# Local attention layers: turned probabilities through a DRAM scratch, four wide reads in place of twelve SBUF copies, and new orders on all engines

## What is computed

```python
def attn_layer(x, Wqkv, qs, ksc, Wo):
    q, k, v = jnp.split(x @ Wqkv, 3, -1)          # 16 heads of 64
    q, k = l2norm(q) * qs, l2norm(k) * ksc
    q = q * cos * scale + rotate_half(q) * sin * scale
    k = k * cos * inv + rotate_half(k) * sin * inv
    out = local_attention(q, k, v)                # window of 64: softmax over this and the last window
    return out @ Wo
def ffn_layer(x, g, bln, W1, b1, W2, b2):
    a, gate = jnp.split((layernorm(x) * g + bln) @ W1 + b1, 2, -1)
    return a * jax.nn.gelu(gate, approximate=False) @ W2 + b2
for i in range(DEPTH):
    x = attn_layer(shift_tokens(x), Wqkv[i], q_scale[i], k_scale[i], Wo[i]) + x
    x = ffn_layer(shift_tokens(x), ln_g[i], ln_b[i], W1[i], b1[i], W2[i], b2[i]) + x
```

## Time and profile before

| | |
|---|---|
| median of 3 runs | 3710.45 us (3704.81 to 3710.89) |
| the profiled execution: time | 3711.28 us |
| the profiled execution: span | 3709.7 us |
| PE busy | 3492.5 us, 94% of the span |
| DVE busy | 2934.3 us, 79% |
| ACT busy | 2244.5 us, 61% |
| POOL busy | 2379.7 us, 64% |
| share of the chain that ended last | PE 62%, DVE 8%, SP's queue 2%, DMA 1% |

### The profile page before, as it was taken

How to read it: one execution, slowest core, us unless ns; L and a number is a source line. 1 busy time by engine, 2 the same in 40 slices (tenths; PEclk the granted TensorE clock), 3 DMA queues, 4 the chain that set the end, 5 groups by cost and what they waited for, 6 DMA issues and landing times.

```text
span 3709.7 us, 78239 instructions
## 1 busy us (share of the span) xinstructions
PE 3492.5 (94%) x25818; PEld 2453.3 (66%) x25818; DVE 2934.3 (79%) x9244; ACT 2244.5 (61%) x6802; POOL 2379.7 (64%) x2088
## 2 busy tenths in 40 slices
...
DMA packets 223105, 277.92 MB, mean 75 GB/s; under 512 B 60624, under 2 KB 184048, under 8 KB 221168
## 3 DMA queue, kind: packets, MB, share of 16 engines
...
q1 hardware_dynamic: 181600, 138.54, 13.1%
...
## 4 chain that ended last, share of the span: by engine, by line
PE 62%; DVE 8%; SPq 2%; issue 1%; POOL 1%; DMA 1%; ACT 0%; DVEq 0%; POOLq 0%; ACTq 0%
PE pj L1857 26%; PE y_ps L1912 9%; PE pj L1929 8%; PE y_ps L1938 7%; PE sc L1885 5%; PE o_ps L1902 4%; PE tp L1865 3%; DVE l_probs L2150 3%; SPq L1701 2%; DVE l_qk_cos L2112 2%; PE tp L1835 1%; DVE l_qT L2046 1%; DVE l_ss L2105 1%; DVE l_hT L2187 0%; DVE l_qk_sin L2114 0%
## 5 line engine op out<-in xcount | busy, mean ns | idle before, releaser
L1857 PE MATMUL pj<-w_qkv,l_xT 128*128 128x512 f32 x2304 | 1082.5, 603 | 48.3 <-DVE l_hT L2187 36.5
L1798 POOL TENSOR_TENSOR l_qk_rot<-l_qk_cos,l_qk_sin 128x512 f32<-128x512 f32 x376 | 580.1, 1543 | 688.3 <-DVE l_qk_sin L2115 565.9
L1857 PEld LDWEIGHTS pj<-w_qkv,l_xT 128*128 128x128 f32 x2304 | 408.5, 191 | 435.7 <-issue 376.6
L511 POOL DMA_INDIRECT f_rows<-in_emb,f_expert x512 | 505.4, 987 | 226.4 <-issue 144.9
L2001 ACT ACTIVATE l_probs<-l_probs,l_low 128x128 f32<-128x128 f32 x1536 | 595.0, 397 | 3.5 <-DVE l_low L2150 2.9
L1929 PE MATMUL pj<-l_xnT,l_w 128*128 128x256 f32 x2112 | 481.9, 380 | 1.2 <-issue 1.2
L1966 ACT ACTIVATE l_qk_raw<-pj 128x512 f32<-128x512 f32 x384 | 228.6, 595 | 398.6 <-DVE l_qk_sin L2115 276.1
L2150 DVE CUSTOM_DVE_ANT_0 l_probs<-sc,l_shut,l_r_q 128x128 f32<-128x128 f32 x1536 | 434.9, 339 | 29.7 <-PE sc L1885 29.0
L1929 PEld LDWEIGHTS pj<-l_xnT,l_w 128*128 128x128 f32 x2112 | 391.6, 191 | 50.6 <-issue 1.8
L1803 POOL TENSOR_TENSOR l_r_q<-l_ssm,l_minus_half 128x8 f32<-128x8 f32 x188 | 370.7, 1972 | 15.7
L2112 DVE TENSOR_TENSOR l_qk_cos<-l_qk_raw,l_rope 128x512 f32<-128x512 f32 x384 | 345.8, 900 | 0.0
...
## 6 DMA issues: line engine op xcount, KB each, us to landing
l_pT<-l_p_turned SPq DMA_DIRECT2D x1728, 32.0 KB, 1.8
w_qkv<-in_L_ffn_Wqkv SPq DMA_DIRECT2D x12, 1024.0 KB, 7.5
...
f_rows<-in_emb,f_expert POOLq DMA_INDIRECT x512
w_o<-in_L_ffn_Wo SPq DMA_DIRECT2D x6, 1024.0 KB, 5.5
w_qkv<-in_L_ffn_Wqkv SPq DMA_DIRECT2D x12, 512.0 KB, 4.9
l_xf<-l_stream SPq DMA_DIRECT2D x48, 128.0 KB, 2.3
```

Source lines behind the costliest of these rows:

```text
L511: pool.indirect_dma_start(rows[:, j % RH, k, :], None, dram["emb"], bass.IndirectOffsetOnAxis(ap=expert[:, n % 2, at:at + 1], axis=0)).the ...
L1798: pool.tensor_tensor(qk_rot[:, i % ROTS, :], qk_cos[:, b, :], qk_sin[:, b, :], ALU.add).then_inc(rotated if s == 0 else pool_front, 1)
L1857: last = pe.matmul(pj[b][:, :], xT[:, k, t * P:(t + 1) * P], w_qkv[:, k, s * INNER + c * 512:s * INNER + (c + 1) * 512], start=(k == 0), s ...
```

## The change

Three things change, all in `local_layers`.

1. The exchange. A new piece `park` writes a whole unit of `p_turned` (all 16 blocks, 512 KB, 4 KB from each of 128 partitions) into a DRAM scratch `parked`, by one DMA. `move` then waits for that DMA (`p_parked`) and reads the blocks back by four DMAs of 128 KB, each into 32 partitions. The zeroing of `pT` and the semaphore `cleared` are gone; masked blocks come as zeros out of the probabilities.
2. What waits for it. `turn` of unit u needs its slot of `p_turned` free: now as soon as the park of unit u - 2 has landed, before when its 12 moves had. `values` waits for 4 DMAs.
3. New lists for all five engines (and a new first pass for DVE). No piece is added or removed but the parks; pieces stand elsewhere.

```diff
-    MOVES = [(a, b, 0) for a, b in ((1, 0), (2, 0), (2, 1), (3, 1), (3, 2), (0, 0), (1, 1), (2, 2), (3, 3))]
-    MOVES += [(a, b, 1) for a, b in ((0, 2), (0, 3), (1, 3))]
-    MOVED = 16 * len(MOVES)
+    MOVED = 16 * 4
...
     ORDER["sync"] = [
-        ("move", 0, -1), ("load_qk", 0, 0), ("stage", 0, -2), ("move", 1, -1), ("load_2", 0, -1), ("load_o", 0, 0), ("load_v", 0, 0),
-        ("load_1", 0, 0), ("move", 2, -1), ("load_cols", 0, 0), ("move", 3, -1),
+        ("move", 0, -1), ("stage", 0, -2), ("park", 1, -1), ("move", 1, -1), ("load_qk", 0, 0), ("load_v", 0, 0), ("park", 2, -1), ("load_1", 0, 0),
+        ("load_2", 0, -1), ("move", 2, -1), ("park", 3, -1), ("load_o", 0, 0), ("move", 3, -1), ("load_cols", 0, 0), ("park", 0, 0),
     ]
...
+        parked = nc.dram_tensor("parked", (2, 4, BLOCK, 4, TILES * UH * BLOCK), F32, kind="Internal").ap()
...
-            def move(n, par, u):
+            def park(n, par, u):
                 sp.wait_ge(turned_32, UNITS * n + u + 1)
                 apart(sp, passed)
-                if n == 0 and u < 2:
-                    sp.wait_ge(cleared, 1)
+                wait(sp, moved[u % 2], MOVED * (2 * n + u // 2))
+                sp.dma_start(parked[u % 2].rearrange("a j b x -> (a j) (b x)"),
+                             p_turned[:, u % 2, :, :, :, :].rearrange("p b t h q -> p (b t h q)")).then_inc(p_parked[u % 2], 16)
+
+            def move(n, par, u):
+                sp.wait_ge(p_parked[u % 2], 16 * (2 * n + u // 2 + 1))
+                apart(sp, passed)
                 wait(sp, o_full, UNITS * n + u - 1)
-                for a, b, t in MOVES:
-                    sp.dma_start(pT[b * BLOCK:(b + 1) * BLOCK, u % 2, a, t:TILES, :, :],
-                                 p_turned[a * BLOCK:(a + 1) * BLOCK, u % 2, b, t:TILES, :, :]).then_inc(moved[u], 16)
+                for b in range(4):
+                    sp.dma_start(pT[b * BLOCK:(b + 1) * BLOCK, u % 2, :, :, :, :].rearrange("p a t h q -> p a (t h q)"),
+                                 parked[u % 2, :, :, b, :].rearrange("a j x -> j a x")).then_inc(moved[u % 2], 16)
...
-                    pool.memset(pT[:, :, :, :, :, :], 0.0).then_inc(cleared, 1)
...
-                pe.wait_ge(moved[u], MOVED * (n + 1))
+                pe.wait_ge(moved[u % 2], MOVED * (2 * n + u // 2 + 1))
...
-                before, unit = (n, u - 2) if u >= 2 else (n - 1, u + 2)
-                wait(dve, moved[unit], MOVED * (before + 1))
+                wait(dve, p_parked[u % 2], 16 * (2 * n + u // 2))
```

More of the change, by code:

```diff
@@ L1415, in local_layers @@
     ORDER["tensor"] = [
-        ("scores", 2, -1), ("project", 5, 0), ("project", 6, 0), ("qk_turn", 1, 0), ("project", 8, 0), ("wo", 0, -2), ("qk_turn", 3, 0),
-        ("project", 7, 0), ("project", 9, 0), ("scores", 3, -1), ("values", 0, -1), ("qk_turn", 2, 0), ("w1", 1, -3), ("w1", 2, -3),
-        ("qk_turn", 5, 0), ("project", 10, 0), ("qk_turn", 4, 0), ("project", 11, 0), ("xs", 0, 1), ("w1", 3, -3), ("w1", 4, -3), ("w1", 5, -3),
-        ("values", 1, -1), ("scores", 0, 0), ("project", 0, 1), ("project", 1, 1), ("qk_turn", 7, 0), ("project", 2, 1), ("xn", 0, -2),
@@ L1420, in local_layers @@
-        ("values", 2, -1), ("scores", 1, 0), ("qk_turn", 6, 0), ("project", 3, 1), ("w2", 0, -3), ("w2", 1, -3), ("qk_turn", 0, 1), ("w1", 0, -2),
-        ("project", 4, 1), ("values", 3, -1),
+        ("scores", 2, -1), ("project", 5, 0), ("project", 6, 0), ("qk_turn", 0, 0), ("qk_turn", 1, 0), ("wo", 0, -2), ("project", 8, 0),
+        ("project", 7, 0), ("qk_turn", 3, 0), ("project", 9, 0), ("qk_turn", 2, 0), ("w1", 1, -3), ("scores", 3, -1), ("values", 0, -1),
+        ("w1", 2, -3), ("project", 10, 0), ("qk_turn", 5, 0), ("project", 11, 0), ("qk_turn", 4, 0), ("xs", 0, 1), ("w1", 3, -3), ("w1", 4, -3),
```

43 lines of the change are left out of this document (23 added, 20 removed).

## The result

| | median | runs | profiled execution | its span |
|---|---|---|---|---|
| before | 3710.03 us | 3704.81 to 3710.89 | 3711.28 us | 3709.7 us |
| after | 3645.64 us | 3643.55 to 3649.63 | 3649.63 us | 3648.1 us |

The ratio is 0.9831, with an interval of 0.9814 to 0.9848: faster by 64 us. Forecast were 3658 us and a range of 3632 to 3700.

What follows compares the result with a forecast made beforehand. PE's own work was taken as the bound (busy 1291.4 of 1316 us), so only its losses between instructions could be won: 3711.3 - 13.5 - 35.1 - 0 - 4 = 3658.7, forecast 3658 us, range 3632 to 3700.

Steps and rivals of the forecast that it cites:

- Steps of 55.9 us: Local layers, `wo` to `wo`: each step falls from 57.0 to 55.9 us, 1.08 us won.
- `w1 1` ahead of `scores 3`, 35.1 us: Ahead of `project 10`: PE's wait for DVE's read-out mostly goes, 0.78 us a step, 35.1 us in 45 steps.
- the 0.29 that was left: Ahead of `project 10`: loss expected to remain each step, 0.19 us of wait plus 0.10 of slow restart.
- `project 8` behind `wo`, 13.5 us: `project 5`'s bank gets all of `wo` more for read-out, so 0.30 us a step goes, 13.5 us in 45 steps.
- The exchange hidden, 0 in the steps: From `turn 2` to `values 2`: 8.2 us of DRAM round trip fits into 11.9 us, 3.7 us of cover, no cost.
- the estimate of 3.2 us from its formula: The park's landing by the skill's formula: 2.0 us plus the bytes at 436 GB/s; the working took 3.7 us.
- the first rival: At `values 2`, every step: DRAM round trip late, slower kernel; 3897 us with landings like a 1024 KB load; chance 0.11.
- Layer ends net 0: Steps at layer ends: 5 us lost to late loads against 5 us of `pT` waits won, net 0.
- The 5 us allowed for a late `load_qk`: `project 0` of a new layer: weights late behind SP's wait for the park, 1 us in each of 5 steps.
- all 7.0 us for `pT`: Full steps' waits for `pT` where a load stands ahead of a `move`: 5 of the 7 us expected to go.
- First and last steps, 4 us: First and last steps: SP spends less time a unit, winning 1 us at the start and 3 at the end.

Runs made afterwards that it cites:

- lists_only: The kernel before with the five new lists, parks struck out, exchange still 12 SBUF copies a unit: 3668.48 us, ratio 0.9891.
- lists_with_old_sp: The kernel before with new lists on PE, DVE, ACT and POOL; SBUF copies and SP's list as before: 3764.95 us against 3805.37, ratio 0.9896.
- exchange_only: The kernel before with the DRAM exchange, old lists on all engines, each park right ahead of its move: 3733.57 us, ratio 1.0062.
- exchange_and_sp_list: The kernel before with the DRAM exchange and SP's new list, the other engines' lists old: 3801.58 us against 3805.37, ratio 0.9989.
- rotate7_between: The changed kernel with `rotate 7` between the two halves of `top 3` on DVE: 3843.92 us against 3805.37 for the kernel before, ratio 1.0096.
- turn5_first: The changed kernel with `qk_turn 5` ahead of `project 10` on PE: 3633.72 us, ratio 0.9795 to the kernel before.
- p8_before_wo: The changed kernel with `project 8` put back ahead of `wo` on PE: 3648.51 us, ratio 0.9835 to the kernel before.
- park_two: The changed kernel with one further 512 KB write to spare DRAM ahead of each park: 3672.64 us, ratio 0.9897 to the kernel before.
- park_five: The changed kernel with four further 512 KB writes to spare DRAM ahead of each park: 4042.68 us against 3805.37 for the kernel before, ratio 1.0613.
- lists_only_again: A repeat, in the third batch, of the kernel before with the new lists and no DRAM exchange: 3668.15 us, ratio 0.9891.
- lists_loads_up: New lists without the DRAM exchange, `load_qk` moved ahead of `move 1`, `load_cols` ahead of `load_o` and `move 3` on SP: 3655.56 us, ratio 0.9857.

## Why the prediction was right, and where it wasn't

- **Steps of 55.9 us.** Right, 55.93. All of it is the lists' (lists_only, lists_with_old_sp: 55.93 without the DRAM exchange; exchange_only, exchange_and_sp_list: 56.99 with it).
- **`w1 1` ahead of `scores 3`, 35.1 us.** Right in mechanism and size. 4.09 us from `scores 3` to `project 10` for 4.05; rotate7_between shows that DVE's order there is what PE waits for, and with turn5_first the step falls by 0.28 of the 0.29 that was left.
- **`project 8` behind `wo`, 13.5 us.** The size was right, the reason not the one that was needed. p8_before_wo takes the place away and loses nothing. The step of the working is "the bank of `project 5` has the whole of `wo` more to be read out in". That is true, but two things that the working left out are each enough without it: the bank is free 0.63 us earlier, since ACT's releaser on DVE is done sooner, and a second turn stands between. The working read PE's list for this place and not what ACT waits for. The three were not tried one by one, so which of them is needed stays open.
- **The exchange hidden, 0 in the steps.** Right: 8.0 us of round trip for 8.2, 4.3 us of cover for 3.7, and park_two's plain steps unchanged with another 512 KB in the way. Inside the round trip two misses cancel: from park to first read 3.6 us pass for 3.7, but from first read to last 1.3 for 2.1, and the last lands 3.0 us later for 2.3. The Trainium skill ("DMA: Bandwidth & Descriptors", Anatomy of one DMA) puts most of a DMA's fixed time into the receipt, heaviest for HBM. That section is about DMAs that GpSimd issues, and these are SP's; even so the estimate of 3.2 us from its formula is close to the 3.0 measured. A price that speaks against the change is not seen in these rows. Of the two transfers only the park writes DRAM, so the first rival's "receipt from DRAM twice" counts one too many.
- **Layer ends net 0.** Mis-sized, they gave 6.1 us. The 5 us allowed for a late `load_qk` were not needed in the changed kernel: no wait at `project 0` is listed. SP is not early: the load goes out 20.0 us after that step's `wo`, not the 13 of the working (PE and SP of the changed kernel, one layer's end):

```profile
2177.10 2.11 PE L1916 MATMUL y_ps<-w_o,l_oT 128*128 128x256 f32 x9
...
2197.08 0.83 SPq L2236 DMA_DIRECT2D w_qkv<-in_L_ffn_Wqkv  x2
...
2207.30 1.98 PE L1861 MATMUL pj<-w_qkv,l_xT 128*128 128x512 f32 x4
```

  `project 0` comes 30.2 us after `wo`, not 23. Both numbers were 7 too low, and the 10 us between them, which decide, were right: the second of the two loads lands at 2204.7, 2.6 us ahead of `project 0`. And all 7.0 us for `pT` went, not 5. exchange_only and park_two show that the place is a real danger: 42 and 24 us of excess.
- **First and last steps, 4 us.** Mis-sized: 9.8 us at the start, where 1 was forecast with 4 to either side, and 2.2 at the end for 3. The last steps take 84.6 us before, 84.8 to 86.1 in the four kernels with the new lists and no DRAM exchange, and 79.4 to 83.6 in those with the exchange (park_five left out), so the end's gain is the exchange's. For the start, counted from the first `project` to the second `wo`: 148.4 us before; 144.9, 144.2, 147.0 and 144.6 with the new lists alone; 143.8 and 143.8 with the exchange and the old lists of the other engines; 137.7 to 141.3 in the five with both. So the lists win 1.4 to 4.2 us there, the exchange 4.6, and both together 7 to 11. The working had 1 us of it, from SP's time for a unit, and left the lists an unknown. Chance lies ahead of the first `project`: lists_only and lists_only_again are one kernel, and it starts at 910.42 and 917.68 in them. In the two traces compared here it took 3.1 us back.

In sum: the profiled execution was to take 3658.7 us and took 3649.63. Of those 9.1 us 6.1 are layer ends and 8.8 the start, less 3.1 ahead of the local layers, 2.0 in the steps (44 of 1.06 us for 45 of 1.08) and 0.8 at the end. The median is another 4 us below the profiled execution, so 12 us separate it from the forecast of 3658.

**What the parts are worth.** The lists alone 42 us (0.9891), the exchange alone minus 23 (1.0062), with SP's list about plus 4 (0.9989, not told from nothing), both 64 (0.9831). They don't add up, since each changes what the other costs. On top of the lists the exchange brings 0.9891 - 0.9831 = 0.60%, 22 us. Of these 0.34%, 13 us, can be had without it by moving the loads (lists_loads_up). The other 0.26%, 10 us, stand between intervals that still touch (0.984 to 0.9873 and 0.9814 to 0.9848). They fit the first and last steps: 144.6 us from the first `project` to the second `wo` for 138.6, and 85.6 us for the last steps for 82.3, with `pT` waits of 7.2 and 6.7 us for 0.8 and 1.2. That the difference is these was read from the traces and not tried apart.

**Open.** Which of the three reasons frees `project 8`. What slows the 1408 KB load to 9.1 us. When a wait of PE brings the lower clock: in exchange_only it follows the waits of 4.3 to 4.8 us and one of 2.0, and not the one of 2.98, and in rotate7_between it follows 5 of the 44 waits of 1.9 us.
